# Relation rows: the gathered rows in four slots of 14 columns in place of two of 28

## The reference, cut to what matters

```
h_proj = einsum('nd,rde->rne', h, relation_weight)   # 32 relations
t_r = h_proj[etype, src]
h_r = h_proj[etype, dst]
att = sum(t_r * tanh(h_r + efeat), -1)
...
msg = h[src] * softmax_over_dst(att)
```

## Time and profile before

| | |
|---|---|
| three runs, median (lowest to highest) | 9190.53 us (9164.67 to 9205.76) |
| profiled execution, its own time | 9157.66 us |
| span of its trace | 9156.1 us |
| mean granted TensorE clock | 0.608 |
| busy over the span: PE, DVE, ACT, POOL | 42%, 58%, 27%, 41% |

### The profile page before, as it was taken

The page is one execution under the profiler, slowest core; times in us unless marked ns, Lnnn a source line. Parts: engine busy times, 40 slices in busy tenths (PEclk is TensorE's granted clock), DMA queues, the critical chain, the costliest instruction groups (busy, mean ns, idle before and its releaser), DMA issues. The chain is left out here.

```text
span 9156.1 us, 102588 instructions
## 1 busy us (share of the span) xinstructions
PE 3846.7 (42%) x24601; PEld 3085.2 (34%) x24602; DVE 5285.9 (58%) x8989; ACT 2454.3 (27%) x3870; POOL 3780.2 (41%) x4315
## 2 busy tenths in 40 slices
PE   5455555520017881444443232222249522222196
PEld 2444444520017881333333210000048300000186
DVE  5454445569742112444444468888856588888675
ACT  4333333321622221433333221111112111111121
POOL 4444444400020004444444236666625166666261
PEclk8555555555558995666666555555579555555596
DMA  7565556677737881222222366666645477666462
GB/s 291 152 186 174 170 179 186 184 212 194 284 67 266 293 281 52 82 83 80 93 80 81 44 179 183 184 183 184 171 99 132 128 183 185 182 183 183 107 139 69
DMA packets 1551900, 1462.17 MB, mean 160 GB/s; under 512 B 1296593, under 2 KB 1344365, under 8 KB 1535296
## 3 DMA queue, kind: packets, MB, share of 16 engines
q1 hardware_dynamic: 966152, 807.40, 28.8%
q0 software_dynamic: 175712, 462.09, 19.3%
q10 hardware_dynamic: 409944, 191.70, 7.4%
HBM read 1078.30 MB, written 381.40 MB: 159 GB/s over the span
## 5 line engine op out<-in xcount | busy, mean ns | idle before, releaser
L2328 POOL DMA_INDIRECT rows_p<-node_rows,stage_i x1728 | 1637.9, 948 | 1090.7 <-issue 842.8
L2359 PE MATMUL psZ<-parts_r,hot_t 126*128 x1728 | 629.5, 468 | 1948.7 <-issue 966.3
L2359 PEld LDWEIGHTS psZ<-parts_r,hot_t 126*128 126x128 bf16 x1728 | 181.0, 105 | 2398.1 <-issue 2378.1
L715 PE MATMUL psP<-window,pair_hot 128*128 x3136 | 725.6, 420 | 579.4 <-issue 349.9
L790 DVE SCALAR_TENSOR_TENSOR pair_run<-pair_run,same_c,psP 128x64 f32<-128x64 f32 x1568 | 440.1, 281 | 871.9 <-remote 743.4
L2416 DVE TENSOR_TENSOR psZ<-psZ,rows_p 128x660 f32<-128x660 f32 x864 | 724.7, 846 | 357.7 <-issue 236.5
L715 PEld LDWEIGHTS psP<-window,pair_hot 128*128 128x128 f32 x3136 | 690.8, 329 | 626.7 <-issue 626.7
L257 POOL DMA_INDIRECT rows_s<-hpx,stage_i x784 | 748.5, 955 | 264.7 <-issue 242.7
L257 POOL DMA_INDIRECT both<-table,stage_i x784 | 742.9, 948 | 264.0 <-issue 242.6
L2423 DVE SCALAR_TENSOR_TENSOR lz<-psZ,att 128x660 f32<-128x660 f32 x864 | 723.0, 837 | 95.1 <-issue 69.1
L2429 DVE TENSOR_REDUCE sc<-lz 128x10 f32<-128x660 f32 x864 | 711.9, 831 | 59.4 <-issue 45.1
(11 more groups left out here) (523 smaller groups left out, 8016.2 us busy)
## 6 DMA issues: line engine op xcount, KB each, us to landing
tile<-adj SPq DMA_DIRECT2D x228, 781.2 KB, 4.8
x_src<-rows_p SPq DMA_DIRECT2D x288, 192.0 KB
xs<-x_src SPq DMA_DIRECT2D x432, 128.0 KB, 3.1
locs<-loc_rows SPq DMA_DIRECT2D x144, 378.0 KB
hpx<-stage ACTq DMA_DIRECT2D x25, 2048.0 KB
pair_loc<-pair_locs SPq DMA_DIRECT2D x28, 1792.0 KB
window<-hpx SPq DMA_DIRECT2D x196, 256.0 KB
dst_runs<-pair_run SPq DMA_DIRECT2D x28, 1792.0 KB
```

Source lines behind the costliest of these rows:

```text
L715: last = pe.matmul(psP[:, n % 2, j * D:(j + 1) * D], hot[:, n % 2, j * CE:(j + 1) * CE], window[:, n % 2, bass.ds(rel[j], 1), :].rearrange ...
L2328: pool.indirect_dma_start(rows[:, k, j, :], None, g.node_rows, bass.IndirectOffsetOnAxis(stage[:, k, j:j + 1], 0)).then_inc(got[k], 16)
L2359: last = pe.matmul(psZ[:, n % 4, j, 0:ZH], hot[:, k, col * CE:(col + 1) * CE], parts[:, bass.ds(at[col], 1), :].rearrange("p o c -> p (o c)"),
```

## The change

`rows_s` gets four slots of 14 columns (same size in all), and `stage_i` too. The slots are stored by ACT after batches 3, 6, 10 and 13 of a turn. The indices of a slot are no longer copied by POOL. They come by a DMA of their own, from `hpST` (also in SBUF), issued by SP for the first turn and after that by ACT just ahead of the slot's two stores. POOL waits for that load and the two stores, then issues 14 gathers. The chunks of the pairs, the tiles and all their loops stay as they are, and so does the number of gathered rows and bytes.

```diff
+    SLOTS = 4
+    KS = 2 * K // SLOTS
+    SLOT_AT = {3: 0, 6: 1, 10: 2, 13: 3}
...
-        stage, rows = s.sb("stage_i", [P, 2, K], i32), s.sb("rows_s", [P, 2, K, 2 * D])
+        stage, rows = s.sb("stage_i", [P, SLOTS, KS], i32), s.sb("rows_s", [P, SLOTS, KS, 2 * D])
...
+                for k in range(SLOTS):
+                    sp.dma_start(stage[:, k, :], g.hpST[:, k * KS:(k + 1) * KS]).then_inc(index_in[k], 16)
                 load_locs(0, 0)
...
                 with pool.Fori(0, NCH // 2) as i:
-                    c.begin(i, 2)
-                    for k in range(2):
+                    for k in range(SLOTS):
+                        pool.wait_ge(index_in[k], i * 16 + 16)
                         pool.wait_ge(t_out[k], i * 16 + 16)
                         pool.wait_ge(x_out[k], i * 16 + 16)
-                        gather_columns(pool, g.hpx, 2 * D, g.hpST, stage, rows, c, i, k, got, staged)
-                c.end(NCH // 2)
+                        pool.sem_inc(staged, 1)
+                        for j in range(KS):
+                            pool.indirect_dma_start(rows[:, k, j, :], None, g.hpx,
+                                                    bass.IndirectOffsetOnAxis(stage[:, k, j:j + 1], 0)).then_inc(got[k], 16)
...
-                        if m == M - 1:
-                            x = i * 2 + k
-                            act.wait_ge(got[k], i * (16 * K) + 16 * K)
-                            act.dma_start(g.t_rows.rearrange("p (j c) -> p j c", c=D)[:, bass.ds(x * K, K), :],
-                                          rows[:, k, :, 0:D]).then_inc(t_out[k], 16)
-                            act.dma_start(g.x_src.rearrange("(j p) c -> p j c", p=P)[:, bass.ds(x * K, K), :],
-                                          rows[:, k, :, D:2 * D]).then_inc(x_out[k], 16)
+                        if n in SLOT_AT:
+                            slot = SLOT_AT[n]
+                            at = i * (SLOTS * KS) + slot * KS
+                            act.wait_ge(got[slot], i * (16 * KS) + 16 * KS)
+                            if not last:
+                                act.dma_start(stage[:, slot, :], g.hpST[:, bass.ds(at + SLOTS * KS, KS)]).then_inc(index_in[slot], 16)
+                            act.dma_start(g.t_rows.rearrange("p (j c) -> p j c", c=D)[:, bass.ds(at, KS), :],
+                                          rows[:, slot, :, 0:D]).then_inc(t_out[slot], 16)
+                            act.dma_start(g.x_src.rearrange("(j p) c -> p j c", p=P)[:, bass.ds(at, KS), :],
+                                          rows[:, slot, :, D:2 * D]).then_inc(x_out[slot], 16)
```

More of the change, by code:

```diff
@@ L632, in relation_rows @@
         psP = s.ps("psP", [P, 2, BP * D])
-        got = [s.pool_sem(g, k) for k in range(2)]
+        got = [s.pool_sem(g, k) for k in range(SLOTS)]
         two = lambda name: [s.sem(f"{name}{k}") for k in range(2)]
-        locs_in, window_in, run_out, t_out, x_out = (two(n) for n in ("locs_in", "window_in", "run_out", "t_out", "x_out"))
-        dve_c, copied, staged, numbered, laned, told = (
-            s.sem(n) for n in ("dve_c", "copied", "staged", "numbered", "laned", "told"))
+        slots = lambda name: [s.sem(f"{name}{k}") for k in range(SLOTS)]
+        locs_in, window_in, run_out = (two(n) for n in ("locs_in", "window_in", "run_out"))
+        t_out, x_out, index_in = (slots(n) for n in ("t_out", "x_out", "index_in"))
+        dve_c, staged, numbered, laned, told = (s.sem(n) for n in ("dve_c", "staged", "numbered", "laned", "told"))
         paired, neared, hot_ready, chained = (s.sem(n) for n in ("paired", "neared", "hot_ready", "chained"))
@@ L690, in _ @@
             def _(pool):
-                c = Chain(pool, copied)
                 pool.iota(lane_i[:, :], pattern=[[1, 1]], base=0, channel_multiplier=-1).then_inc(numbered, 1)
                 with pool.Fori(0, NCH // 2) as i:
-                    c.begin(i, 2)
-                    for k in range(2):
+                    for k in range(SLOTS):
+                        pool.wait_ge(index_in[k], i * 16 + 16)
                         pool.wait_ge(t_out[k], i * 16 + 16)
                         pool.wait_ge(x_out[k], i * 16 + 16)
-                        gather_columns(pool, g.hpx, 2 * D, g.hpST, stage, rows, c, i, k, got, staged)
-                c.end(NCH // 2)
+                        pool.sem_inc(staged, 1)
+                        for j in range(KS):
+                            pool.indirect_dma_start(rows[:, k, j, :], None, g.hpx,
+                                                    bass.IndirectOffsetOnAxis(stage[:, k, j:j + 1], 0)).then_inc(got[k], 16)
             @block.tensor
```

## The result

The changed kernel takes 9151.90 us (five runs, 9143.32 to 9156.97), the kernel before 9183.72 us in five runs beside it (9164.67 to 9205.76). The ratio is 0.9962, with an interval of 0.9944 to 0.9979. That is a gain of 32 us in 9184 by the medians and of 35 us, 0.38%, by the ratio, where 134 us were forecast. It lies in the range given, which reached over no change, and inside the 0.5% that I had called no change.

The account below looks back on a forecast made before the run. The stage was taken as bound by waits, PE's instructions and signals getting through slowly while POOL gathers. 9157.66 - 140 + 5 = 9023 us for the profiled execution, 32.9 under the median, so 9056 forecast; range 8890 to 9240.

Parts of the forecast that it names:

- the blocks would partly join: Four-slot gather blocks on POOL: half of the pairs taken as apart, saving 5.4 us a half turn, 140 us.
- A block of 35.0 us costs 24.6, so its first 10.4 us are free: POOL's gather block: delays begin after 10.4 us, so two separate blocks of 14 lose 13.8 us in place of 24.6.
- both ends that I gave (10.4 and 14.5): Free us per gather block: 10.4, or 14.5 if the missing locations' load explains 4.1; the latter saves 387 us.
- the slower rival: Short gaps before POOL's gather blocks leave less than 10.4 us free; at 3 us free, 104 us slower, 9295; chance 0.20.
- My last sentence: Forecast wrong altogether if the stall is tied to the unchanged number of gathers in a half turn, not block length.
- The saving of 5.4 us a half turn: Gather stalls in the stage: half of the block pairs stay apart, 140 us saved in all.
- The 5 us for the first turn: SP's four first-turn index loads shift later windows 1.5 us and the first gather 0 to 10.3; charged 5 us once.
- my bound of 1.9: ACT's `x_src` store issue: 1.9 us in place of 3.77 if it follows the bytes, so the sum stays 106 us.
- my 5.6 to 11.1: Time from a slot's store to its gather block with half the bytes: between 5.6 and 11.1 us, taken as 8.
- the sign of being right: In the changed profile, DVE's remote waits fall from 743 to 600 us or less.
- The Trainium skill's fixed part for each DMA: Store to gather: 2.0 us fixed per DMA, 52 us less gain over 26 half turns; left out of the sum.
- the second rival: All gather blocks join end to end, so no change: 9190, within 20 us for ACT's added issues; chance 0.23.

Follow-up runs that it names:

- two slots with the pause of 90 numbers: Kernel before plus one POOL addition of 90 numbers after each gather, gathers 1.52 us apart, nothing left out: 8763.81 us beside 9299.14, ratio 0.9426.

## Why the prediction was wrong

**What was right.** The mechanism of the stall: PE's instructions and its signals get through slowly while POOL gathers, and neither POOL's time nor bandwidth does it. The kernels without gathers, with and without a busy POOL, and those with half the bytes show it. That the blocks would partly join was right in size too: half of 26 pairs is 13, and 11 joined.

**The step that failed** is "A block of 35.0 us costs 24.6, so its first 10.4 us are free", carried over to a block of 14. By the same reckoning (35.7 us for a half turn without gathers, 71.4 for a turn) the turns without a join, 112.9 us, pay 41.5 us for four blocks, 10.4 us each. So 6.9 of 17.3 us are free where I had 10.4, and a pair that stays apart costs 20.8 us where I had 13.8. The turns with both pairs joined pay 127.5 - 71.4 = 56.1 us, 28.0 a pair, where I had 24.6, the price of the old block. So the pairs that stayed apart saved 3.9 us each in place of 10.8, and the joined ones lost 3.4, for a reason that the runs don't show. These are estimates from three and two turns. The kernel with four slots alone on a stalling chip has 116.4 to 117.1 us without a join, 111.1 to 119.4 with one and 121.4 to 130.5 with two, so its joins are dear too, and its pairs apart save even less (2.0 us each).

The free part is not a fixed lead that each block has. With the 38.2 us of the kernel without gathers for a base, a block of 28 costs 22.1 us and leaves 12.9 free, a block of 14 that has the rest of a half turn to itself costs 8.3 and leaves 9.0, and one that stays apart in the changed kernel costs 9.1. So most of the free part went with the block's length, and only a little with the shorter gap ahead of it. By the gather that is 0.79, 0.59 and 0.65 us, nearer to a price for each gather than to a free lead. I had read the lead from one length of block at one spacing of gathers, and both ends that I gave (10.4 and 14.5) came from that same pair of half turns. Against the slower rival I had set that ACT waited only 10.17 us after a short gap in rows 11. That compares single waits of one engine, not what a block costs the stage.

What stands in its place: gathers at up to 1.36 us from one to the next slow PE, at 1.52 they hardly do, and the change leaves all 784 of them back to back, 1.25 us apart. That it would leave both their distance and their number as they were could be read from the edit, and that this matters took the experiments. My last sentence had it nearly: wrong altogether if the stall goes by the number of gathers. It goes by their rate first and, at a rate that stalls, roughly by their number, and both are unchanged.

**Point by point.** The saving of 5.4 us a half turn was 1.1 (120.7 to 118.5 us a turn, forecast 110). The 5 us for the first turn were 10. The last turn gained 16.5 us, where I had given it nothing of its own: only one block of 14 falls into it (from 1795.09 us), where one of 28 did. Its first half takes 42.7 us and its last, without gathers, 35.9 as forecast, so this one block costs 6.8 us, which is the size that I had taken for all. An `x_src` issue takes 0.74 us, below my bound of 1.9: half the bytes took a fifth of the time. An index load's issue is 0.49, not 0.378 us; the loads alone change nothing (1.0004), so they were hidden as said, on a chip without the stall. Landing fell from 10.3 to 5.5 us, and from store to first gather it is 9.4 us at 855.81, within my 5.6 to 11.1. The gap ahead of a block fell from 23.64 to 9 to 15 us in the blocks shown. PE's wait for `pair_hot` was 73 us after 79. DVE's remote wait of 428 was under the 600 I had named as the sign of being right, and it misled: most of the rest moved to "PE psP". As a sign I should have taken the sum of DVE's waits for PE under any name, 804 before and 752 after, or the matmuls in a fixed stretch, 2141 and 2188 between 400 and 1,200 us.

The Trainium skill's fixed part for each DMA ("DMA: Bandwidth & Descriptors", "Anatomy of one DMA — SWDGE (gpsimd) path") would have taken 52 us of the gain. The page has that figure for transfers issued by GpSimd, and these stores are issued by ACT. An estimate by that page is 3.1 us for 448 KB and 4.1 for 896 KB, and the trace doesn't agree, for the landing fell from 10.3 to 5.5 us, nearly with the bytes. No run here separates a fixed part from the rest of the gain, and on the chip without the stall splitting alone gained 50 us.

**The rivals.** None came out as told. By its time the result is nearest the second rival (no change, 9190), by its mechanism it is a mixture: pairs apart whose blocks have less than 10.4 us free (6.9, above the 5.0 at which the slower rival breaks even), and joined pairs that cost more than one old block. That the time lies in my range is owed to the range's width and not to the mechanism.

## What to carry to other kernels

When one engine's instructions slow another's through something that the trace doesn't name, change the rate and the number separately before changing the size of blocks: half the work, once at the same distance and once at twice the distance, takes two experiments and tells the two apart. On a stalling chip a pause of 0.26 us at each gather gave 5.7%, fifteen times what the change gave. On a chip without the stall the kernels with such pauses took 1.4% and 3.3% longer than the kernel before. So time both kernels on the same chip, and on more than one, before keeping either. A wait that shrinks counts as a gain only once its neighbours' sum has shrunk with it.

## What the runs showed of the hardware

The same kernel takes 9184 to 9299 us on some chips and 7688 to 7708 on others. Whether PE is slowed by indirect transfers 1.26 us apart differs between them, and the program alone doesn't decide it. The granted clock is 0.50 in the stage on both kinds. What carries the delay, and whether two chips lack it always or lacked it in their one session, stays open: no run here reaches it. Nor is it settled where between 1.36 and 1.52 us the edge is, or if it moves with how many gathers precede it.

Which of the versions tried is best depends on it. Where there is the stall it is two slots with the pause of 90 numbers, 8763.81 against 9299.14 us. Where there is none it is the four slots alone, 7657.26 against 7707.67, with the whole change at 7669.78 not clearly behind. No kernel was shown to be best on both, but the first of these two wasn't timed on a chip without the stall.

A gather holds POOL for 0.92 to 0.96 us with 128 or 64 rows and with 512 or 256 bytes a row, and makes as many packets in each case. Issuing a strided store of 448 KB takes ACT 0.74 us in the changed kernel and one of 896 KB 3.77 in the kernel before (medians of each trace), so issue time isn't in proportion to bytes. In the kernels with four slots on chips without the stall the smaller one's median is 0.87 to 1.15 us.
